# A DLRM tower on one core: an eleventh one-hot table, spread ids kept in SBUF, and gathers in bursts of three

## The reference

```python
e = stack([tbl_f[ids[:, f]] for f in range(26)], axis=1)      # (2048, 26, 128) float32
combined = concatenate([e, r_dense_x[:, None, :]], axis=1)    # 27 features of 128
z = einsum('bfd,bgd->bfg', combined, combined)[:, TRIU_I, TRIU_J]   # 351 products of pairs
h = concatenate([z, r_dense_x], axis=1)                       # (2048, 479)
h = maximum(h @ W_top1 + b_top1, 0)                           # 512
h = maximum(h @ W_top2 + b_top2, 0)                           # 256
y = h @ W_top3                                                # (2048, 1)
```

## Time and profile before

| | |
|---|---|
| runs | 549.79, 554.01, 555.29 us; median 554.01 |
| the profiled execution | 551.39 us, span 549.5 us |
| TensorE busy | 476.3 us of the span |
| VectorE, ScalarE, GpSimd busy | 315.8, 233.9, 248.9 us |
| granted TensorE clock, mean | 0.957 of full |

### The profile page before, as it was taken

The page is one execution under the profiler, slowest core; times in us unless marked ns, Lnnn a source line. Parts: engine busy times, 40 slices in busy tenths (PEclk is TensorE's granted clock), DMA queues, the critical chain, the costliest instruction groups (busy, mean ns, idle before and its releaser), DMA issues.

```text
span 549.5 us, 9188 instructions
## 1 busy us (share of the span) xinstructions
PE 476.3 (87%) x3544; PEld 436.3 (79%) x3544; DVE 315.8 (57%) x503; ACT 233.9 (43%) x755; POOL 248.9 (45%) x266
## 2 busy tenths in 40 slices
PE   3786677998888998899898998989998898899988
PEld 3676576897887888789788888879897887889977
DVE  6994137564467535675366654775367543676252
ACT  3532225443444343534435344443545335354454
POOL 6435554455555554455545445554554545420000
PEclk9998569899899998999999999999999899999999
DMA  8551111111111111111111111111111101100000
GB/s 291 189 151 40 37 38 34 39 39 48 35 39 35 44 39 35 39 38 44 35 35 38 35 49 40 39 35 43 35 40 35 39 24 40 35 21 0 1 2 1
DMA packets 12511, 25.80 MB, mean 47 GB/s; under 512 B 4931, under 2 KB 6603, under 8 KB 12458
## 3 DMA queue, kind: packets, MB, share of 16 engines
q0 software_dynamic: 8192, 16.79, 11.5%
q1 hardware_dynamic: 4276, 8.42, 4.8%
...
## 4 chain that ended last, share of the span: by engine, by line
PE 71%; DVE 10%; DMA 6%; POOL 5%; issue 5%; ACT 2%; another core or an unknown queue 1%; POOLq 0%; DVEq 0%; ACTq 0%
PE x_ps L437 23%; PE gram_ps L453 23%; PE tail_ps L508 13%; DVE onehot L617 8%; DMA raw<-in_tbl,ids_sb 6%; POOL raw L398 4%; PE x_ps L415 4%; PE ids_ps L423 3%; PE tail_ps L478 2%; DVE gram L279 2%; PE tail_ps L487 2%; PE tail_ps L514 2%; DVE split_weights L638 1%; ACT xt L552 0%
## 5 line engine op out<-in xcount | busy, mean ns | idle before, releaser
L398 POOL DMA_INDIRECT raw<-in_tbl,ids_sb x256 | 245.6, 959 | 234.7 <-DMA raw<-in_tbl,ids_sb 161.4
L617 DVE TENSOR_TENSOR onehot<-ids_ps,row_no 128x1024 fp32r<-128x1024 f32 (+1 forms) x160 | 206.7, 1303 | 77.3 <-PE x_ps L437 50.1
L437 PE MATMUL x_ps<-onehot,hot_hi 128*128 128x256 f32 x688 | 185.0, 302 | 24.3 <-DVE onehot L617 17.7
L437 PE MATMUL x_ps<-onehot,hot_lo 128*128 128x256 f32 x688 | 174.4, 286 | 0.0
L437 PEld LDWEIGHTS x_ps<-onehot,hot_hi 128*128 128x128 f32 x688 | 133.3, 194 | 33.2 <-issue 16.4
L453 PE MATMUL gram_ps<-xt 128*128 128x108 f32 x1024 | 137.6, 289 | 14.1 <-DVE gram L279 11.2
L453 PEld LDWEIGHTS gram_ps<-xt 128*128 128x128 f32 x1024 | 129.7, 203 | 21.6 <-ACT gram L279 13.9
L279 DVE COPY gram<-gram_ps 32x104 f32<-32x104 f32 x256 | 68.6, 268 | 117.1 <-PE gram_ps L453 99.7
L437 PEld LDWEIGHTS x_ps<-onehot,hot_lo 128*128 128x128 f32 x688 | 133.6, 194 | 0.0
L279 ACT COPY gram<-gram_ps 32x104 f32<-32x104 f32 x256 | 60.4, 236 | 103.0 <-PE gram_ps L453 73.3
L552 ACT COPY xt<-x_ps 128x256 f32<-128x256 f32 x80 | 49.7, 621 | 99.7 <-PE x_ps L437 91.4
...
## 6 DMA issues: line engine op xcount, KB each, us to landing
raw<-in_tbl,ids_sb POOLq DMA_INDIRECT x256, 2.5
table_home<-in_tbl SPq DMA_DIRECT2D x4, 512.0 KB, 8.8
...
raw<-in_tbl SPq DMA_DIRECT2D x2, 512.0 KB, 4.7
...
h<-in_tbl SPq DMA_DIRECT2D x1, 512.0 KB, 11.2
...
```

The costliest lines, as they stand in the source:

```text
L398: nc.gpsimd.indirect_dma_start(out=raw[k][:, f, :], out_offset=None, in_=tables[f], in_offset=bass.IndirectOffsetOnAxis(ap=ids_sb[:, t, f: ...
L437: last = nc.tensor.matmul(ps, table[:, chunk_at[j] + c, :], onehot[:, p % RING, c - a, :], start=(c == 0 and table is hot_hi), stop=(c == ...
L617: nc.vector.tensor_tensor(onehot[:, p % RING, 0:n, :], ids_ps[:, it % 2, :].unsqueeze(1).to_broadcast([P, n, BLOCK]), row_no[chunks[it % n ...
```

## The change

It has these parts.

- `HOT` goes from 10 to 11: one more table of 1250 rows (10 chunks) is looked up by one-hot, 15 tables stay cold. A block has 22 pieces for 20 and 30 gathers for 32.
- Gathers are numbered through all tiles. Before each burst of `BURST` = 3 GpSimd waits for the first two gathers of the burst before it, and no longer for the third. Its waits for free raw places (`turn_full`) stay.
- ScalarE copies each spread pair from `ids_ps` to `ids_wide` in SBUF (two pairs deep), and VectorE compares from there. The spread of a pair stands in the order two pairs ahead and waits only for the copy before it.
- The ids are loaded and rounded per block (`ids_load`, `ids_round`) into full 128 partitions, and `pick` is the identity with one column repeated.
- `RING` goes from 2 to 3, `DENSE` from 3 to 2, `y_sb` has one buffer.
- The tail steps are spread by `TAIL_OVER` = 3 over the pieces and the first three gram steps instead of ending in a lump.
- VectorE takes `zt_lo` straight from PSUM, so the whole `zt` and its copy go, and the PSUM bank is freed by VectorE.
- The last part of `W_top2` is loaded into `h1` once the first weights are split.
- The scratch for the gathers' descriptors is halved.

```diff
-HOT = 10
+HOT = 11
 RAW = 2
-DENSE = 3
-RING = 2
+DENSE = 2
+RING = 3
 PIECE = 5
 EARLY = 2
+BURST = 3
 
 COVER = {"cols": 2.0, "zt": 1.0, "h1": 0.2, "h2": 0.15, "y": 0.25}
...
-SPREAD = 1.2
+TAIL_OVER = 3
...
+    def is_last(t, f):
+        return (t * nf + f) % BURST == BURST - 1
+
+    def lead_count(t, g, upto=None):
+
+        fs = turn_groups[g]
+        full = len([f for f in fs if not is_last(t, f)])
+        return t // RAW * full + len([f for f in fs if not is_last(t, f) and (upto is None or f <= upto)])
+
+    def last_count(t, g):
+        return (t // RAW + 1) * len([f for f in turn_groups[g] if is_last(t, f)])
...
+            steps += [("ids", pair) for pair in range(2, -(-items // 2)) if p == ids_pair_end(pair - 2)]
             steps.append(("hot", p))
-            for pair in range(1, -(-items // 2)):
-                if p == ids_pair_end(pair - 1) - RING:
-                    steps.append(("ids", pair))
         return steps
...
-        scale = SPREAD * n / tail_at[-1] if tail_of else 0
+        scale = (n + TAIL_OVER) / tail_at[-1] if tail_of else 0
+        left = [(at * scale, step) for step, at in zip(tail_of, tail_at)]
         ends = [i for i in range(n) if first + i + 1 in item_end]
         turn_at = [ends[(g + 1) * len(ends) // n_turn - 1] for g in range(n_turn)]
         steps = []
         for i in range(n):
-            steps += [step for step, at in zip(tail_of, tail_at) if i - 1 < at * scale <= i]
+            while left and left[0][0] <= i:
+                steps.append(left.pop(0)[1])
             steps += hot_steps(first + i, first + i + 1)
             steps += [turn for turn, at in zip(turns[0], turn_at) if at == i]
-        steps += [step for step, at in zip(tail_of, tail_at) if at * scale > n - 1]
-        assert len([s for s in steps if s[0] == "tail"]) == len(tail_of)
         m = h * gram_block
         for i in range(n_gram):
+            while left and left[0][0] <= n + i:
+                steps.append(left.pop(0)[1])
             steps += turns[1][i * n_turn // n_gram:(i + 1) * n_turn // n_gram]
             steps.append(("gram", m + i))
+        assert len([s for s in steps if s[0] == "tail"]) == len(tail_of)
         m += n_gram
...
-    first_steps = [("ids", 0)] + hot_steps(0, item_end[EARLY - 1])
+    first_steps = [("ids", 0), ("ids", 1)] + hot_steps(0, item_end[EARLY - 1])
...
-        ids_row = sb("ids_row", [nh, batch], F32R)
-        pick = sb("pick", [nh, nh, P], F32R)
+        ids_raw = sb("ids_raw", [P, BLOCK], I32)
+        ids_row = sb("ids_row", [P, 2, BLOCK], F32R)
+        ids_wide = sb("ids_wide", [P, 2, 2, BLOCK])
+        pick = sb("pick", [P, P], F32R)
...
-        table, part = 8 * P, 10 * P
-        homes = [(0, 0), (0, table), (1, 0), (1, part), (1, 2 * part), (1, 3 * part), (2, 0), (3, 0), (1, 0), (1, part)][:nh]
+        homes = [(0, 0)] + [(1, 10 * P * n) for n in range(5)] + [(2, 0), (3, 0)] + [(1, 10 * P * n) for n in (5, 0, 1)]
+        homes = homes[:nh]
...
-                 zt[:, :, :].rearrange("p k n -> p (k n)")[:, 0:2 * d2]]
+                 h1[:, 0:2, :].rearrange("p m n -> p (m n)")]
...
-                last = copy(zt[0:kz[j], j, :].rearrange("p (g s) -> p g s", s=QUAD), src)
+                return
...
-            if kind in ("zt", "h1"):
-                bank = tail_bank[key]
+            bank = tail_bank[key]
+            if kind == "zt":
+                dve.wait_ge(zt_rounded, h * n_kz + j + 1)
+                src = tail_ps[bank][0:kz[j], 0:BLOCK].rearrange("p (s g) -> p g s", s=QUAD)
+                hi, lo = (part[0:kz[j], j, :].rearrange("p (g s) -> p g s", s=QUAD) for part in (zt_hi, zt_lo))
+                nc.vector.tensor_tensor(lo, src, hi.bitcast(F32), ALU.subtract).then_inc(zt_split, 1)
+                dve.wait_ge(zt_split, h * n_kz + j + 1)
+                dve.sem_inc(tail_copied[bank], 1)
+            elif kind == "h1":
                 dve.wait_ge(tail_copied[bank], h * tail_per[bank] + tail_nth[key] + 1)
-                rows, whole, hi, lo, split = ((kz[j], zt, zt_hi, zt_lo, zt_split) if kind == "zt" else
-                                              (P, h1, h1_hi, h1_lo, h1_split))
-                nc.vector.tensor_tensor(lo[0:rows, j, :], whole[0:rows, j, :], hi[0:rows, j, :].bitcast(F32),
-                                        ALU.subtract).then_inc(split, 1)
+                nc.vector.tensor_tensor(h1_lo[:, j, :], h1[:, j, :], h1_hi[:, j, :].bitcast(F32),
+                                        ALU.subtract).then_inc(h1_split, 1)
 
         @block.sync
...
+            def ids_load(h):
+                sp.dma_start(ids_raw[0:nh, :], hot_ids[:, h * BLOCK:(h + 1) * BLOCK]).then_inc(ids_raw_in, 16)
+
             sp.dma_start(ids_sb[:, :, :], ids).then_inc(ids_in, 16)
-            sp.dma_start(ids_row_in, hot_ids).then_inc(ids_row_landed, 16)
+            sp.wait_ge(ids_raw_cleared, 1)
+            ids_load(0)
...
                 if j == EARLY:
                     dense_load(0)
+                    sp.wait_ge(ids_row_ready, 1)
+                    ids_load(1)
...
+            for k, landed in ((0, weights_in), (1, rest_weights_in)):
+                if k == 1:
+                    for h in range(1, DENSE):
+                        dense_load(h)
+                    sp.wait_ge(weights_split, 1)
                 sp.dma_start(w2_in[k].rearrange("p (k n) -> p k n", k=2),
-                             w2.rearrange("(k p) n -> p k n", p=P)[:, 2 * k:2 * k + 2, :]).then_inc(weights_in, 16)
-            for h in range(1, DENSE):
-                dense_load(h)
+                             w2.rearrange("(k p) n -> p k n", p=P)[:, 2 * k:2 * k + 2, :]).then_inc(landed, 16)
             for h in range(blocks):
+                if h + 2 < blocks:
+                    sp.wait_ge(ids_row_ready, h + 2)
+                    ids_load(h + 2)
                 if h + DENSE < blocks:
                     sp.wait_ge(tail_full["h1"], (h + 1) * m1)
                     sp.wait_ge(dense_copied, h + 1)
                     dense_load(h + DENSE)
                 sp.wait_ge(y_copied, h + 1)
-                sp.dma_start(out[:, h * BLOCK:(h + 1) * BLOCK], y_sb[0:1, h % 2, :]).then_inc(y_stored[h % 2], 16)
...
-                    if g > 0:
-                        pool.wait_ge(rows_in[k][g - 1], (t // RAW + 1) * (16 * (len(turn_groups[g - 1]) - 1)))
-                        pool.wait_ge(last_in[k][g - 1], (t // RAW + 1) * 16)
-                    elif t > 0:
-                        pool.wait_ge(rows_in[(t - 1) % RAW][n_turn - 1],
-                                     ((t - 1) // RAW + 1) * (16 * (len(turn_groups[n_turn - 1]) - 1)))
-                        pool.wait_ge(last_in[(t - 1) % RAW][n_turn - 1], ((t - 1) // RAW + 1) * 16)
                     for f in fs:
+                        n = t * nf + f
+                        if n % BURST == 0:
+                            for lead in range(max(n - BURST, 0), n - 1):
+                                tl, fl = divmod(lead, nf)
+                                pool.wait_ge(lead_in[tl % RAW][fl // 4], 16 * lead_count(tl, fl // 4, fl))
                         nc.gpsimd.indirect_dma_start(
                             out=raw[k][:, f, :], out_offset=None, in_=tables[f],
                             in_offset=bass.IndirectOffsetOnAxis(ap=ids_sb[:, t, f:f + 1], axis=0),
-                        ).then_inc(last_in[k][g] if f == fs[-1] else rows_in[k][g], 16)
+                        ).then_inc(last_in[k][g] if is_last(t, f) else lead_in[k][g], 16)
...
-                pe.wait_ge(rows_in[k][g], (t // RAW + 1) * (16 * (len(turn_groups[g]) - 1)))
-                pe.wait_ge(last_in[k][g], (t // RAW + 1) * 16)
+                pe.wait_ge(lead_in[k][g], 16 * lead_count(t, g))
...
-                if pair > 0:
-                    pe.wait_ge(piece_ready, ids_pair_end(pair - 1))
+                reach(pe, ids_copied, pair)
+                pe.wait_ge(ids_row_ready, min(2 * pair + 1, items - 1) // nh + 1)
                 for it in range(2 * pair, min(2 * pair + 2, items)):
                     h, j = divmod(it, nh)
-                    last = nc.tensor.matmul(ids_ps[:, it % 2, :], pick[:, j, :],
-                                            ids_row[:, h * BLOCK:(h + 1) * BLOCK], start=True, stop=True)
+                    last = nc.tensor.matmul(ids_ps[:, it % 2, :], pick[:, j:j + 1].to_broadcast([P, P]),
+                                            ids_row[:, h % 2, :], start=True, stop=True)
                 last.then_inc(ids_full, 1)
 
...
+            def ids_copy(pair):
+                act.wait_ge(ids_full, pair + 1)
+                if pair > 1:
+                    act.wait_ge(piece_ready, ids_pair_end(pair - 2))
+                copy(ids_wide[:, pair % 2, :, :], ids_ps[:, :, :]).then_inc(ids_copied, 1)
+
...
+                        for n, (hi, _, src) in enumerate(weight_parts):
+                            if n == len(weight_parts) - 1:
```

(25 more changed lines are left out.)

50 lines of the change are left out of this document (25 added, 25 removed).

## The result

The changed kernel took 521.13 us (median of 516.06, 516.12, 526.15 and 529.99), the kernel before beside it 552.68. The ratio is 0.934, interval 0.925 to 0.943. The forecast was 533 with a range of 517 to 562: the direction was right and the size too small, 3.8% against 6.6%, and the two shorter executions lie just under the range. Repeats on other chips gave another size: 0.929 on a second chip; on a third 509.3 against 514.5 us by the medians, 1%, and 500.6 against 512.3 by the shortest executions, 2%.

What follows compares the result with a forecast made beforehand. Block 0 was taken to wait for gathers, steady blocks to be bound by TensorE with short stalls. From 551.4 us, -8 + 2.5 - 7 x 2.1 - 0.5 = -20.7 gave 530.7, median 533, range 517 to 562.

Steps and rivals of the forecast that it cites:

- Eleventh table, +2.4 a block: TensorE, each block: 20 added matmuls at 0.12 us cost 2.4 us; removed transposes and added ids cancel within 0.2.
- Stalls that come back, 4.7 a block: TensorE, steady blocks: shorter waits for pieces, ids and last-layer weights, hidden overlap and clock together return 4.7 us per block.
- Bursts buy nothing in steady blocks: Steady blocks: bursts of three cut gathers to 46.8 us per block, no gain there since gathers are not last.
- w = 0.35 us a gather: Gathers: each waits on average 0.35 us for the end of a VectorE operation with two SBUF inputs.
- the decision point: Steady blocks: gathers pass TensorE's 61.6 us per block once w is over 0.74 us, twice the estimate.
- Gathers hold back the pieces: Rival, VectorE: pieces starting inside a gather wait for its end, 4.9 us per block; median 551 or 568; chance 0.06.
- Block 0, -8: Block 0: the last burst's third gather lands near 64 us against 72.14, -8 us, from -11 to -2.
- Late W_top2, +2.5: First dense step: W_top2's last part loads after the weight split, so it comes 1.7 to 4 us later; +2.5 once.
- Tail over the products, a gain of 0.7: TensorE, steady blocks: the last layer's wait moves into the products, where there is other work; 0.7 us per block.
- Half of the missing 2% of clock: TensorE, steady blocks: the missing clock is 1.3 us per block; fewer stalls return half, 0.65.
- The bounds: Steady blocks: net gain 2.1 us, from +2.6 (nothing comes back) to -5.4 (6.0 + 0.55 + 1.3 come back).
- two rivals, 566 and 547: 566: TensorE feels all of the held-back pieces, chance 0.06; 547: bursts without effect, half the steady gain gone, chance 0.05.

Runs made afterwards that it cites:

- group 1's variant: The changed kernel with the comparison reading spread ids from PSUM and the spread waiting for the preceding pair's pieces: 520.8 us, steady block 59.8 us.
- the burst kernel: The kernel before, groups of four gathers waiting for the preceding group's first three: 595.5 us, ratio 1.071; with plain loads for gathers 492.4 us.
- the early load: The changed kernel with the last part of W_top2 loaded before block 0: 517.2 us, beside 517.4 for the changed kernel.
- the lump and the early weights: The changed kernel with leftover tail steps in a lump before the products and W_top2's last part loaded early: 497.6 us, ratio 0.966; repeated, 497.2 us.
- ten tables: The changed kernel with ten one-hot tables and bursts of four waiting for three: 532.8 us; with full descriptor scratch 540.4 us.

## Why the prediction was right in direction and wrong in size

- *Eleventh table, +2.4 a block*: right for its 20 matmuls, which follow each other at 0.12 us as said. What the prediction let cancel to within 0.2 us did not: the spread of a pair, in the kernel before and in the changed one (both without late completions), with the matmuls beside it.

```profile
262.22 0.27 PE L437 MATMUL x_ps<-onehot,hot_lo 128*128 128x256 f32 x1
262.43 0.50 PE L423 MATMUL ids_ps<-ids_row,pick 10*128 10x256 f32 x2
262.85 0.58 PE L453 MATMUL gram_ps<-xt 128*128 128x108 f32 x3
```

```profile
267.43 0.27 PE L468 MATMUL x_ps<-onehot,hot_lo 128*128 128x256 f32 x1
267.54 0.40 PE L454 MATMUL ids_ps<-ids_row,pick 128*128 128x256 f32 x2
267.78 0.28 PE L468 MATMUL x_ps<-onehot,hot_hi 128*128 128x256 f32 x1
```

  A pair with its neighbours took 0.63 us with the ids on 10 partitions and takes 0.35 on 128, 5 x 0.63 against 5.5 x 0.35, 1.2 us less per block. By this estimate the work grew by 1.0 us a block (2.4, less 0.2 for two transposes and 1.2). It is 0.35 us too in group 1's variant that reads the ids from PSUM (257.38 to 257.73), so the copy is not what does it; whether the partitions or the new form of `pick` does, no run separates.
- *Stalls that come back, 4.7 a block*: this is the step that failed. On the first chip 6.8 came back (63.3 + 1.0 - 57.5), on the chips without late completions 2.2 (57.3 + 1.0 - 56.1). The forecast read the waits of the earlier trace rows as the kernel's own order. But TensorE's idle time was 5.8 us a block on the first chip (316.5 - 287.7 over five) and 1.6 without late completions (286.5 - 278.5), with the same schedule. Its waits in the five steady blocks, first with late completions and then without:

```profile
PE gram_ps L453 <- DVE gram L279: 8.0, 9, 2.1
PE x_ps L437 <- DVE onehot L617: 7.9, 9, 1.6
PE ids_ps L423 <- DVE onehot L617: 4.9, 7, 1.6
```

```profile
PE x_ps L437 <- DVE onehot L617: 3.8, 10, 0.4
PE ids_ps L423 <- DVE onehot L617: 3.5, 9, 0.4
```

  The wait for gram copies is gone, and the longest others shrink from 1.6 to 0.4 us. The 6.0 us between the two blocks (63.3 and 57.3) go with completions that were late while gathers were under way. It is a comparison across chips for this kernel; on one chip with late completions the changed kernel's and the burst kernel's blocks without gathers (56.1 and 57.2) are those of the chips without. The gram phases hold half of it (22.6 us against 19.6 on average over five blocks), the piece phases the rest. The changed kernel pays 1.4 us (57.5 against 56.1), 1.3 of them in its gram phases (21.5 against 20.2). That split is shown. That its two pairs of spread ids and three pieces take up the rest is argued: no run undoes both where completions are late. Why completions come late is open.
- *Bursts buy nothing in steady blocks*: right for the kernel before, whose block is 57.2 us with and without them when the loads are plain, and wrong by what it left out. Without them the copied ids make gathers a bound (60.6 us a block), and alone, where completions are late, they cost 7%.
- *w = 0.35 us a gather*: 0.25 measured (1.197 - 0.95), and the decision point was far off. The mean was the wrong quantity: the estimate took it that a gather waits for one operation, and it can be held through eleven.
- *Gathers hold back the pieces*: pieces of 1222 and 1488 ns, as before, speak against it, and nothing for it.
- *Block 0, -8*: the last turn of tile 1 came at 68.52 for 72.14, -3.6, as gathers of up to 1.97 us stood between pieces; yet the stretch to block 1's products gained 11.2. The granted clock there was 0.88 for 0.80; what else gained was not taken apart.
- *Late W_top2, +2.5*: a wait of 5.65 us, of which the early load removed 2.2; the total didn't move.
- *Tail over the products, a gain of 0.7*: wrong in sign. With the lump and the early weights, which alone changed nothing, a block took 55.8 us for 56.1 on the chips without late completions.
- *Half of the missing 2% of clock*: all of it came back in the steady blocks (0.98 to 1.00), and where no completions were late the kernel before had 1.00 too. So the lower clock goes with the late completions; that they bring it about is inferred.
- *The bounds*: -5.4 a block adds up to -5.3 (6.0 + 0.55 + 1.3 - 2.6), and two rivals, 566 and 547, to 565 and 546; nothing hangs on it.

Open: what in a gather delays TensorE's completions, and why in some groups alone; why more gathers in a bunch (bursts on the kernel before, ten tables) make it so much worse; and what the eleventh table is worth by itself where completions are not late, since ten tables were run only where they were.
